# Linear attention in a kernel of many stages: weighted sums turned round, denominators repeated by columns of ones

## The reference, cut to what matters

```python
def _phi(x, omega):
    proj = jnp.einsum('bhnd,md->bhnm', x, omega)
    norm = 0.5 * jnp.sum(x * x, axis=-1, keepdims=True)
    return jnp.exp(proj - norm) / math.sqrt(M)
...
kv_cumsum = jnp.cumsum(kv, axis=2)
k_cumsum = jnp.cumsum(phi_k, axis=2)
out = jnp.einsum('bhnm,bhnmd->bhnd', phi_q, kv_cumsum)
z = 1.0 / (jnp.einsum('bhnm,bhnm->bhn', phi_q, k_cumsum) + 1e-06)
out = out * z[..., None]
...
return out @ wo.T + bo
```

## Time and profile before

| | us |
|---|---|
| median of three runs (lowest, highest) | 4367.74 (4365.59, 4370.99) |
| the profiled execution | 4368.54 |
| its span in the trace | 4366.7 |
| this stage in the trace | 777.0 to 1418.2 |

### The profile page before, as it was taken

The page is one execution under the profiler, slowest core; times in us unless marked ns, Lnnn a source line. Parts: engine busy times, 40 slices in busy tenths (PEclk is TensorE's granted clock), DMA queues, the critical chain, the costliest instruction groups (busy, mean ns, idle before and its releaser), DMA issues. The chain is left out here.

```text
span 4366.7 us, 117087 instructions
## 1 busy us (share of the span) xinstructions
PE 4132.9 (95%) x40848; PEld 2923.2 (67%) x40848; DVE 2432.7 (56%) x7468; ACT 1864.6 (43%) x4849; POOL 775.6 (18%) x3244
## 2 busy tenths in 40 slices
PE   6998999999999999999899999899999798989999
PEld 4555777777787455555555788787878455666666
DVE  5775665455554788887455444666666555531111
ACT  3433443333332466565233222566666453233333
POOL 1111221000000477666122000111111210000000
PEclk9999999999999999999899999999999998989999
DMA  1000000000000000000000000000000100000000
GB/s 57 0 0 26 1 0 1 27 0 0 0 0 0 11 2 2 1 1 1 36 0 0 4 0 0 2 3 3 3 3 3 56 0 1 0 1 6 3 5 8
DMA packets 4096, 29.02 MB, mean 7 GB/s; under 512 B 432, under 2 KB 944, under 8 KB 2352
## 3 DMA queue, kind: packets, MB, share of 16 engines
q1 hardware_dynamic: 3776, 24.97, 1.5%
HBM read 22.87 MB, written 2.10 MB: 6 GB/s over the span
## 5 line engine op out<-in xcount | busy, mean ns | idle before, releaser
L604 DVE TENSOR_REDUCE cells_row_max<-banks 128x4 f32<-128x512 f32 x384 | 238.3, 682 | 161.8 <-PE banks L397 161.8
L2361 ACT ACTIVATE experts_hidden<-banks,weights 128x512 f32<-128x512 f32 x256 | 175.8, 687 | 262.9 <-PE banks L2303 261.3
L761 PE MATMUL banks<-clock_fill 128*128 128x512 bf16 x900 | 275.8, 394 | 1.2 <-PEq L101 1.2
L2311 PEld LDWEIGHTS banks<-weights,experts_hidden 128*128 128x128 f32 x2048 | 238.6, 192 | 30.1 <-issue 30.1
L2381 DVE SCALAR_TENSOR_TENSOR experts_acc<-banks,experts_gate,experts_acc 128x128 f32<-128x128 f32 x224 | 63.1, 344 | 348.3 <-PE banks L2311 348.3
L2303 PE MATMUL banks<-act_a,weights 128*128 (+1 forms) x512 | 244.9, 609 | 11.8 <-PEq L101 11.1
L541 ACT ACTIVATE cells_probs<-banks 128x512 f32<-128x512 f32 x384 | 198.3, 603 | 98.4 <-PE banks L437 90.0
L2311 PE MATMUL banks<-weights,experts_hidden 128*128 128x128 f32 x2048 | 238.8, 274 | 0.0
L604 DVE TENSOR_REDUCE attn_row_max<-banks 128x4 f32<-128x512 f32 x256 | 158.8, 682 | 133.2 <-PE banks L397 133.2
L1582 ACT ACTIVATE wave_hidden_turned<-banks,weights 128x128 f32<-128x128 f32 x512 | 206.6, 460 | 38.4 <-PE banks L1526 36.2
L2579 ACT ACTIVATE lin_context_turned<-banks 128x256 f32<-128x256 f32 x128 | 49.1, 384 | 402.7 <-PE banks L2531 402.7
(11 more groups left out here) (552 smaller groups left out, 10101.1 us busy)
## 6 DMA issues: line engine op xcount, KB each, us to landing
weights<-in_p SPq DMA_DIRECT2D x1, 2894.5 KB, 16.9
weights<-in_p SPq DMA_DIRECT2D x1, 2894.0 KB, 9.5
weights<-in_p SPq DMA_DIRECT2D x2, 1396.0 KB, 7.6
x_res<-in_x SPq DMA_DIRECT2D x1, 2048.0 KB, 15.3
out_x<-x_res SPq DMA_DIRECT2D x8, 256.0 KB, 2.0
weights<-in_p SPq DMA_DIRECT2D x1, 1836.0 KB, 10.9
weights<-in_p SPq DMA_DIRECT2D x1, 1835.5 KB, 6.9
weights<-in_p SPq DMA_DIRECT2D x1, 1344.5 KB, 9.9
```

What stands on the lines that cost most here:

```text
L604: dve.tensor_reduce(mt[:, 4 * g:4 * g + 4], bank, AX_X, ALU.max).then_inc(s["max_ready"], 1)
L761: pe.matmul(core.ps[:, bank, :], core.fill[:, 0:P], core.fill[:, :], start=True, stop=True)
L2311: last = pe.matmul(ps[:, OUT + e % 2, t * P:(t + 1) * P], hs[:, e % 2 * DEPTH + f, t * P:(t + 1) * P], w("W2", (e * DEPTH + f) * P, P), st ...
L2361: act.activation(hs[:, e % 2 * DEPTH + f, :], ps[:, f % 2, :], ACT.Gelu, bias=w("b1", j, 1)).then_inc(s["h_ready"], 1)
```

## The change

In `sums` the operands change places: the values of a head are now the stationary operand, 128 columns wide, of which 64 are the values and 64 are ones, and the masked weights are the moving operand (128 columns). A head's result then has its 64 context columns on 64 partitions and the denominator, repeated, on the other 64, and each token is a column. The two heads of a pair put values and ones in opposite halves, so that the context lands where `ot` wants it. `turn`, its copy on ScalarE and two semaphores are gone. ScalarE takes over the copy of the values (two instructions of 128x128) and reads the sums in four instructions of 64x256: denominators with 1e-6 added (Identity with a bias), moved to the other half of the partitions, and weighted sums. VectorE's `normalise`, now for step k-4, is a reciprocal of 128x256 and a product of 128x256, both from SBUF, ahead of `mask`. The buffer of the values is filled with ones at the stage's start, and ScalarE waits for that. `output` waits for the product directly.

```diff
@@ -2415,15 +2415,16 @@
         qk = sb("qk", [P, 2, BANK])
         sq = sb("square", [P, 2, BANK])
         phi = sb("features", [P, 2, 2, 2, P])
-        vt = sb("value", [P, 4, HEADS, DH + 1])
+
+        vt = sb("value", [P, 4, HEADS, P])
         sm = sb("masked", [P, 2, 2, 2, P])
-        den = sb("denominator", [P, HEADS])
-        inv = sb("inverse", [P, HEADS])
-        o = sb("context", [P, 2, 2, P])
-        ot = sb("context_turned", [P, NJ, P])
+        den = sb("denominator", [P, 2, 2, P])
+        ct = sb("weighted", [P, 2, 2, P])
+        inv = sb("inverse", [P, 2, P])
+        ot = sb("context", [P, NJ, P])
         s = {n: sem(n) for n in ["source_ready", "ones_ready", "qk_done", "qk_ready", "sq_ready", "phi_done", "phi_ready",
-                                 "v_done", "v_ready", "s_done", "s_masked", "sum_done", "den_ready", "inv_ready",
-                                 "context_ready", "ct_done", "ct_ready", "out_done", "out_read"]}
+                                 "v_done", "v_ready", "s_done", "s_masked", "sum_done", "sum_read", "inv_ready",
+                                 "context_ready", "out_done", "out_read"]}
         block = ctx.enter_context(nc.Block())
 
         def run(eng, body):
@@ -2513,28 +2514,21 @@
                 last.then_inc(s["s_done"], 1)
 
             def sums(st):
+
                 pe.wait_ge(s["s_masked"], st.n + 1)
                 pe.wait_ge(s["v_ready"], st.n + 1)
-                past(pe, s["context_ready"], st.n)
+                past(pe, s["sum_read"], st.n)
                 for h in range(HEADS):
                     a, half = h // 2, h % 2 if h < 2 else 3 - h
-                    last = pe.matmul(ps[:, SUMS, h * (DH + 1):(h + 1) * (DH + 1)], sm[:, st.m % 2, half, a, :],
-                                     vt[:, st.m % 4, h, :], start=True, stop=True)
+                    last = pe.matmul(ps[:, SUMS, h * P:(h + 1) * P], vt[:, st.m % 4, h, :],
+                                     sm[:, st.m % 2, half, a, :], start=True, stop=True)
                 last.then_inc(s["sum_done"], 1)
 
-            def turn(st):
+            def output(st):
                 pe.wait_ge(s["context_ready"], st.n + 1)
-                past(pe, s["ct_ready"], st.n)
-                if st.m == 0:
-                    past(pe, s["out_read"], st.u)
-                for a in range(2):
-                    last = pe.transpose(ps[:, OUT, a * P:(a + 1) * P], o[:, st.m % 2, a, :], const("ident"))
-                last.then_inc(s["ct_done"], 1)
-
-            def output(st):
-                pe.wait_ge(s["ct_ready"], st.n + 1)
+                past(pe, s["out_read"], st.u)
                 for j in range(NJ):
-                    last = pe.matmul(ps[:, OUT, 2 * P:3 * P], w("woT", j * P, P), ot[:, j, :], start=(j == 0),
+                    last = pe.matmul(ps[:, OUT, 0:P], w("woT", j * P, P), ot[:, j, :], start=(j == 0),
                                      stop=(j == NJ - 1))
                 last.then_inc(s["out_done"], 1)
 
@@ -2543,8 +2537,6 @@
                     features_wait(p[1])
                 if p[0] is not None:
                     project(p[0])
-                if p[4] is not None:
-                    turn(p[4])
                 if p[1] is not None:
                     features(p[1])
                 if p[2] is not None:
@@ -2572,39 +2564,48 @@
                 act.activation(phi[:, st.m % 2, :, :, :].rearrange("p a t j -> p a (t j)"), ps[:, PHI:PHI + 2, 0:2 * P],
                                ACT.Exp, bias=const("ln_m")).then_inc(s["phi_ready"], 1)
 
-            def turned(st):
-                act.wait_ge(s["ct_done"], st.n + 1)
-                if st.m == 0:
-                    past(act, s["out_done"], st.u)
-                act.activation(ot[:, 2 * st.m:2 * st.m + 2, :], ps[:, OUT, 0:2 * P].rearrange("p (a j) -> p a j", a=2),
-                               ACT.Copy).then_inc(s["ct_ready"], 1)
+            def value(st):
+                act.wait_ge(s["v_done"], st.n + 1)
+                past(act, s["sum_done"], st.n - 3)
+                for hh in range(2):
+                    last = act.activation(
+                        vt[:, st.m % 4, hh::2, DH * hh:DH * (hh + 1)],
+                        ps[:, VAL, 0:2 * P].rearrange("p (h d) -> p h d", h=HEADS)[:, hh::2, :], ACT.Copy)
+                last.then_inc(s["v_ready"], 1)
+
+            def read_sums(st):
+                act.wait_ge(s["sum_done"], st.n + 1)
+                past(act, s["context_ready"], st.n - 1)
+                total = ps[:, SUMS, :].rearrange("p (a h j) -> p a h j", a=2, h=2)
+                for hh in range(2):
+                    own, other = DH * hh, DH * (1 - hh)
+                    act.activation(den[own:own + DH, st.m % 2, :, :], total[other:other + DH, :, hh, :], ACT.Identity,
+                                   bias=const("eps6", rows=DH, first=other))
+                    last = act.activation(ct[own:own + DH, st.m % 2, :, :], total[own:own + DH, :, hh, :], ACT.Copy)
+                last.then_inc(s["sum_read"], 1)
 
             def body(p):
-                if p[4] is not None:
-                    turned(p[4])
                 if p[0] is not None:
                     square(p[0])
                 if p[1] is not None:
                     features(p[1])
-
+                if p[0] is not None:
+                    value(p[0])
+                if p[3] is not None:
+                    read_sums(p[3])
+
+            act.wait_ge(s["ones_ready"], 1)
             run(act, body)
 
         @block.vector
         def _(dve):
             wait_pack(dve, core, 2)
-            dve.memset(vt[:, :, :, DH:DH + 1], 1.0).then_inc(s["ones_ready"], 1)
-            dve.wait_ge(s["ones_ready"], 1)
+            dve.memset(vt[:, :, :, :], 1.0).then_inc(s["ones_ready"], 1)
 
             def query_key(st):
                 dve.wait_ge(s["qk_done"], st.n + 1)
                 past(dve, s["phi_done"], st.n - 1)
                 dve.tensor_copy(qk[:, st.m % 2, :], ps[:, QK, :]).then_inc(s["qk_ready"], 1)
-
-            def value(st):
-                dve.wait_ge(s["v_done"], st.n + 1)
-                past(dve, s["sum_done"], st.n - 3)
-                dve.tensor_copy(vt[:, st.m % 4, :, 0:DH], ps[:, VAL, 0:2 * P].rearrange(
-                    "p (h d) -> p h d", h=HEADS)).then_inc(s["v_ready"], 1)
 
             def mask(st):
                 dve.wait_ge(s["s_done"], st.n + 1)
@@ -2614,35 +2615,28 @@
                     [P, 2, 2, P]), ALU.mult).then_inc(s["s_masked"], 1)
 
             def normalise(st):
-                n = st.n
-                dve.wait_ge(s["sum_done"], n + 1)
-                total = ps[:, SUMS, 0:HEADS * (DH + 1)].rearrange("p (h d) -> p h d", h=HEADS)
-                past(dve, s["inv_ready"], n)
-                dve.tensor_scalar(den[:, :], total[:, :, DH], 1.0e-6, None, ALU.add).then_inc(s["den_ready"], 1)
-                dve.wait_ge(s["den_ready"], n + 1)
-                past(dve, s["context_ready"], n)
-                dve.reciprocal(inv[:, :], den[:, :]).then_inc(s["inv_ready"], 1)
-                dve.wait_ge(s["inv_ready"], n + 1)
-                past(dve, s["ct_done"], n - 1)
-                dve.tensor_tensor(o[:, st.m % 2, :, :].rearrange("p a (h d) -> p (a h) d", h=2), total[:, :, 0:DH],
-                                  inv[:, :].unsqueeze(2).broadcast_to([P, HEADS, DH]), ALU.mult).then_inc(
-                    s["context_ready"], 1)
+                dve.wait_ge(s["sum_read"], st.n + 1)
+                past(dve, s["context_ready"], st.n)
+                dve.reciprocal(inv[:, :, :], den[:, st.m % 2, :, :]).then_inc(s["inv_ready"], 1)
+                dve.wait_ge(s["inv_ready"], st.n + 1)
+                if st.m == 0:
+                    past(dve, s["out_done"], st.u)
+                dve.tensor_tensor(ot[:, 2 * st.m:2 * st.m + 2, :], ct[:, st.m % 2, :, :], inv[:, :, :],
+                                  ALU.mult).then_inc(s["context_ready"], 1)
 
             def output(st):
                 dve.wait_ge(s["out_done"], st.u + 1)
                 xb = core.x[:, tok(st.u * P, P)]
-                dve.scalar_tensor_tensor(out=xb, in0=ps[:, OUT, 2 * P:3 * P], scalar=w("bo"), in1=xb, op0=ALU.add,
+                dve.scalar_tensor_tensor(out=xb, in0=ps[:, OUT, 0:P], scalar=w("bo"), in1=xb, op0=ALU.add,
                                          op1=ALU.add).then_inc(s["out_read"], 1)
 
             def body(p):
                 if p[0] is not None:
                     query_key(p[0])
+                if p[4] is not None:
+                    normalise(p[4])
                 if p[2] is not None:
                     mask(p[2])
-                if p[0] is not None:
-                    value(p[0])
-                if p[3] is not None:
-                    normalise(p[3])
                 if p[4] is not None and p[4].m == NP - 1:
                     output(p[4])
 
```

## The result

The changed kernel takes 4343.16 us (median of 4 runs, 4337.28 to 4345.28) against 4368.05 (4 runs, 4365.59 to 4370.99). The ratio is 0.9941, with a 95% interval of 0.9923 to 0.9958: 25 us or 0.6% faster, which is more than the 0.2% that the prediction took as the least that can be told from no change. The forecast was 4334, with 4320 to 4354 around it.

The account below looks back on a forecast made before the run. The prediction took TensorE's instruction stream to bound the stage. Bodies -37.8, late product +2.6 and drain +2 gave -33.2 us on the profiled 4368.5, so 4335, and 4334 for the median, range 4320 to 4354.

Parts of the forecast that it names:

- the bodies: TensorE's repeated loop part without output: 4.13 us against a mean of 4.435, saving 0.305 in 124 bodies, -37.8 us.
- the late product: VectorE's product, needed by the output at 4.13 and ready at 4.21, 0.08 late once a sequence: +2.6 us.
- The turn: Transposes leave TensorE; projections to features take 1.03 us, saving 0.42 in three bodies and 0.17 in the fourth.
- Rival 2: TensorE's change of tile size costs what the turn did: features at 1.20, body 4.30, 4355 us; chance 0.06.
- The wider sums: TensorE's sums with 128 moving columns instead of 65: 8 passes take 0.89 us instead of 0.84, 0.05 a body.
- rival 4: TensorE's passes cost by moving columns: widening costs 0.44 a body instead of 0.05, old passes 56 ns, 4382 us; chance 0.02.
- The reciprocal: VectorE's new reciprocal of 128x256, extrapolated from three smaller sizes: 1.75 us, with bounds of 0.42 and about 3.3.
- Rival 1: VectorE's reciprocal takes 2.2 us, so the output waits 0.53 for the product: +14 us, 4348 us; chance 0.13.
- The ends: Start and drain of the stage: the fill of ones (1.8 us) delays nothing, the drain's chain grows by about 2 us.
- The rival on the other side: VectorE becomes the bound, past a reciprocal of 2.66 us; at 3.3 us it costs +43 us, 4410 us; chance 0.06.

Follow-up runs that it names:

- the second series: The changed kernel measured once more with no edit: 4343.48 us, ratio 0.9936 to the kernel before.
- e2_no_turn: The kernel before with the two transposes left out, so the output projection gets the context unturned: 4323.30 us, ratio 0.9894 to the kernel before.
- e1_wide_only: The kernel before with only the moving operand of the sums widened from 65 to 128 columns: 4373.17 us, ratio 1.0009 to the kernel before.
- the delayed kernels: The changed kernel with 1, 2 or 3 fills of 0.91 us on VectorE behind the stage: 4340.90, 4348.28 and 4339.43 us.
- e3_den_first: The changed kernel with ScalarE reading both denominators first, with their own semaphore for VectorE's reciprocal: 4325.89 us, ratio 0.9897 to the kernel before.
- d3_pad3: The changed kernel with three fills (2.7 us) on VectorE behind the changed stage: 4339.43 us, ratio 0.9939 to the kernel before.
- d2_pad2: The changed kernel with two fills (1.8 us) on VectorE behind the changed stage: 4348.28 us, ratio 0.9951 to the kernel before.

## Why the prediction was right, and where it was off

The direction, the bound and the mechanism were right, and the time lies in the range. The gain was 25 us (27 in the second series), where 34 had been forecast. The forecast of the stage alone, 33.2 against 34.7, is closer than its terms: the bodies and the late product are off by 8 and 6 us and offset each other.

**What bounds.** Right: TensorE's instruction stream, before and after. It is busy in all but 0.7 us of the 200 from 1000 to 1200 in the changed kernel.

**The turn.** The prediction took 1.03 from projections to features, with 0.99 as the low bound and 1.20 as the high one; it is 0.99 in the changed kernel and 1.04 in e2_no_turn, where the sums ahead have 65 columns. The row from the filling pipeline gave 0.99. So the body is 4.08 instead of 4.13, and the bodies gave back 45.7 us where the sum has 37.8 (another 1.4 of it is one body in eight that took 4.59 in the kernel before, not 4.50). Rival 2 (1.20) is out.

**The wider sums.** 0.89 as forecast, and e1_wide_only shows them alone. But the 0.05 a body that the sum has for them is given back by the passes behind, which the prediction didn't foresee: bodies take 4.08 with and without them. This is the place where the Trainium skill ("TensorE: Matmul & The Clock Gate", the section on the phases) and the first trace differed: by its number of moving columns the widening would have cost 54 us. Measured are 3.2. Only the first pass of a group took as little time as rival 4 said, 57 ns for 65 columns; the others were held at 112. The same page of the Trainium skill (the section on weight-path perf modes) says that the fast weight load is off for float32; a weight load of 128 float32 columns as the floor of these passes fits that, and so do the loads themselves, which follow at 112 ns with 65 and with 128 columns. But no run changed the load, so the cause is argued and not shown. Rival 4 is out.

**The reciprocal.** 1.75 us forecast from three small rows, 1.751 measured over eight times the largest of them. The estimate of 2.2 us from the repeat count in the Trainium skill ("VectorE: DVE Perf Modes", the 8-slice walkthrough) is too high; the measurement decides. Rival 1 priced a late product at that duration: 0.53 late and 14 us. The reciprocal is faster, and the product was 0.23 late for another reason, the next paragraph's.

**The late product.** Here a size was off, and it hung on the body's: "0.08 late: 32 x 0.08 = +2.6 us". The product was ready 4.18 behind the projections (forecast 4.17), but the body is 4.08, not 4.13, and the output started 0.13 after the product's end, not 0.04; so 0.23 late, and 0.04 more in the output. Together 8.4 us instead of 2.6. That the stage's sum came out all the same is luck: the shorter body saved more and made the product later. A cost that is a difference of two near times has the error of both.

**The ends.** Between the same places of the loop (the projections of the first full body to the last output in the loop) the changed kernel takes 37.3 us less, forecast 35.2. The start of the stage was 1.0 shorter. The drain, from that output to the next stage, went from 17.2 to 20.8 us: +3.6 instead of "+2". The longer chain is about as priced: of the 3.2 us more from the last sums' start to the last output's, 2.2 are the chain. The other 1.0 is the last sums at the lower clock (2.01 instead of 1.00), and the last output takes 0.6 more (3.78 instead of 3.18). This clock is what the prediction left out. It fell before TensorE's long wait for the last product, not in it.

**What failed** is the step that no part of the sum names: -33.2 in the stage was set equal to -33.2 in the whole. In the stage it was 34.7; the rest went behind it. The 9 us between forecast and result are not in any changed instruction. The profiled pair shows 13.4 lost there, and the median over nine runs about 8. The thirteen profiled runs show that it goes with the time at the lower clock, and the delayed kernels speak for its depending on when those stages begin, within the scatter said above. Why the changed kernel lands on the worse side in all its runs, while e3_den_first, 10 us earlier, keeps nearly its whole gain (44.3 of 44.9 us), is open: what sets the moments at which the clock changes wasn't measured.

**The rival on the other side** had the mechanism right and its price wrong. At 1.75 us of reciprocal VectorE is not the bound, at 3.5 it is; the threshold of 2.66 in between wasn't tried. The stage then costs 159 us more, not the 101 that its formula gives, though a body between outputs takes 4.93 and not the formula's 5.34. The formula takes for granted that VectorE works through the output. It can't: the output waits for its product, and its next copy waits for the projections behind the output.

## What to carry to other kernels

When TensorE is the bound, price a change by distances between starts in its timeline and then follow the new chain on the other engines to the instruction that TensorE meets first; here 187 us of VectorE's work cost about 12, all of it at two places, the outputs and the drain. Let a semaphore stand behind the part that the next engine needs, not behind the whole group: splitting one wait gave back about 9 us, a quarter of what the change itself had gained in the stage. In a kernel of many stages, read the changed stage alone before judging by the whole: here unchanged stages took between 2945 and 2962 us in the profiled runs, and between 2949.5 and 2961.8 in three kernels in which only the moment differs at which those stages begin.

## What the runs showed that was not expected

- With 0.9 us more of delay (d3_pad3 against d2_pad2) the kernel was 8.9 us faster in the median, and the profiled run had 40 us less at TensorE's lower clock in stages that are the same.
- Widening the moving operand of the float32 sums from 65 to 128 columns costs 52 ns once in a group of eight passes (57 to 109 ns, the first pass); the others start 112 ns apart in both, as their weight loads do. In the changed kernel nothing of it is left, with bodies of 4.08 as in e2_no_turn.
- An activation of 64 partitions x 256 takes as long as one of 128 x 256 (378 for a Copy, 470 ns for an Identity with bias, against 384 and 475), also where it moves data to the other half of the partitions.
- The product of 128x256 takes 425 ns from SBUF, as it did from the bank (424).
